# First layer's experts of a two-layer gated cross-attention block: one plain fp32 product where three rounded ones stood

## The chip, the cores and the metric

One core of one Trainium2 chip runs the whole program. The metric is device time in microseconds, from several executions of the same program; lower is better. TensorE is PE in the profile (its weight loads are PEld), VectorE is DVE, ScalarE is ACT, GpSimd is POOL and SyncE is SP.

## The reference

Two layers, each a gated cross-attention and a gated feed-forward part, over 4 × 512 tokens of width 256. The change touches the first layer's feed-forward part alone, eight experts of which each token uses one:

```python
x = hidden_states.reshape(-1, d)
router_logits = x @ Wr + br
expert_mask = jax.nn.one_hot(jnp.argmax(router_logits, axis=-1), num_experts, dtype=x.dtype)
out = jnp.zeros_like(x)
for e in range(num_experts):
    h = jax.nn.gelu(x @ W1[e] + b1[e], approximate=False)
    h = jax.nn.gelu(h @ W2[e] + b2[e], approximate=False)
    y = h @ W3[e] + b3[e]
    out = out + expert_mask[:, e:e + 1] * y
```

W1 is 256 × 1024, W2 1024 × 512 and W3 512 × 256 for each expert, everything in fp32.

## The kernel before

The program runs four phases after one another: sigmoid_attention, experts_phase, softmax_attention and last_ffn_phase. In a product of two fp32 matrices it writes each operand as a rounded high half of type float32r and a low half, the rest (x − high), also float32r. mm3 (line 48) then adds three matmuls into one PSUM bank: high × high, high × low, low × high (its lines 50 to 52, under which all phases' products stand in the profile). Where operands aren't split, a product is a single nc.tensor.matmul on fp32 operands; line 608 (probabilities times values, 4 batches × 2 × 4 calls, 512 columns, each into 32 of the array's columns) and line 586 (router logits, 32 calls, 8 columns) of the first attention are of that kind, and so are the transposes.

experts_phase: the router has given every token an expert; the tokens lie in DRAM in buckets (xs), one per expert. The tokens of an expert are cut into slots of 256 rows. PE runs one loop over all slots, in order of the experts; with this input there are 12 slots. The first slot of an expert is here called an opening slot, and an expert with tokens a visit. The other engines loop over the experts, and inside over an expert's slots.

What a slot does, in the order written out for PE in slot (lines 1738 to 1773):
- W1: for each of 8 blocks m of the first hidden layer, 2 products (over 256 inputs) of 256 columns. They go to one of four PSUM banks in turn (RING).
- transpose_slot(s + 1), line 1734: four transposes of the next slot's rows xg.
- W2: for each of 4 blocks, 8 products of 256 columns. For the first block all products with W2's high half come before those with its low half (lines 1756 to 1761), so that the low half may come later.
- W3: for each of 4 blocks of the hidden layer, 2 products of 256 columns, into banks 4 and 5.

ACT writes each of the 12 blocks per slot as h32 = Gelu(PSUM + bias) (line 1566), and the high halves of the transposed rows (gT_hi, line 1582), of three quarters of W1 (line 1593), of W2 (line 1572) and of W3 (line 1576). DVE writes high and low halves of each h block (lines 1633 and 1635), the low half of the rows (gT_lo, line 1618), the first quarter of W1's high half (line 1700) and all low halves of weights (lines 1707, 1641, 1644). The splits of W2 are put at fixed blocks of the opening slot (W2_AT, W3_AT), those of W1 for the next expert behind the last slot of the present one. DVE also adds the last bias to the result in finish (line 1627), at block 9 of the following slot or, for an expert's last slot, behind the split of W1. POOL fetches the rows xg of slot s + 1 once slot s's rows are transposed (line 1517), fetches b3 and stores the results (line 1521). SP loads the raw weights of a visit as soon as the last visit's have been split (lines 1483, 1490, 1492); in the last visit it loads w1_raw once more (line 1497) and copies the second layer's weights inside DRAM (fw, line 1501). The phase ends when all of them are done.

Of the kernel before, what the change touches and what calls it, by code (L numbers as in the profile page):

```python
# [1412 lines left out]
def experts_phase(nc, k, io):  # L1413
# [4 lines left out]
    with ctx:  # L1418
# [18 lines left out]
        b3_ld, zero_ok, w1q_ok, fw_st = sem("b3_ld"), sem("zero_ok"), sem("w1q_ok"), sem("fw_st")  # L1437
# [4 lines left out]
        gT_hi, gT_lo = sb("gT_hi", [P, C, SLOT], F32R), sb("gT_lo", [P, C, SLOT], F32R)  # L1442
        h32 = sb("h32", [P, RING, SLOT])
        h_hi, h_lo = sb("h_hi", [P, BL, SLOT], F32R), sb("h_lo", [P, BL, SLOT], F32R)
        yo = sb("yo", [P, HALVES, D])
        b_ld, w1_ld, w3_ld, xg_ld, y_st = (sem(n) for n in ("b_ld", "w1_ld", "w3_ld", "xg_ld", "y_st"))
        w1h_ok, w1l_ok, w2h_ok, w2l_ok, w3h_ok, w3l_ok = (sem(n) for n in ("w1h_ok", "w1l_ok", "w2h_ok", "w2l_ok", "w3h_ok", "w3l_ok"))
        gt_done, gh_ok, gl_ok, hb_done = (sem(n) for n in ("gt_done", "gh_ok", "gl_ok", "hb_done"))

        gelu_ok, hh_ok, hl_ok, y_done, y_used = (sem(n) for n in ("gelu_ok", "hh_ok", "hl_ok", "y_done", "y_used"))
# [23 lines left out]
        def _(sp):  # L1476
            sp.dma_start(b12[:], io["b12"]).then_inc(b_ld, 16)
            sp.wait_ge(meta_ok, 3)
            with sp.Fori(0, E0) as e:
                n0, n1, v = slots_of(nc, sp, meta, e, SLOTS0)  # L1480
                with sp.If(n0 < n1):
                    sp.wait_ge(w1l_ok, v * W1Q + 1)
# [3 lines left out]
                    for h in range(2):  # L1486

                        sp.wait_ge(w2l_ok, v * M2 + (h + 1) * M2 // 2)
                        cols = slice(h * M2 // 2, (h + 1) * M2 // 2)
                        sp.dma_start(w2_raw[:, cols], io["W2"][bass.ds(e * P, P), cols]).then_inc(w2_ld[h], 16)  # L1490
                    sp.wait_ge(w3l_ok, v + 1)
# [4 lines left out]
            sp.wait_ge(w1l_ok, visits * W1Q + 1)  # L1496
# [64 lines left out]
        def _(act):  # L1561
            def slot(s, v=None):
                for m in range(BL):
                    act.wait_ge(hb_done, s * BL + m + 2)
                    act.wait_ge(hl_ok, s * BL + m + 1)
                    nc.scalar.activation(h32[:, m % RING], ps[:, HIDDEN_BANKS[m % RING], 0:SLOT], ACT.Gelu,  # L1566
                                         bias=be[:, m:m + 1]).then_inc(gelu_ok, 1)
                    if v is not None and m in W2_AT:
                        i = W2_AT.index(m)
                        if i % 2 == 0:  # L1570
                            act.wait_ge(w2_ld[i // 2], 16 * v + 16)
                        nc.scalar.activation(w2_hi[:, i], w2_raw[:, i], ACT.Copy).then_inc(w2h_ok, 1)
# [11 lines left out]
            act.sem_inc(gelu_ok, RING)  # L1584

# [13 lines left out]
            with act.Fori(0, E0) as e:  # L1599
                n0, n1, v = slots_of(nc, act, meta, e, SLOTS0)  # L1600
                with act.If(n0 < n1):
                    nc.scalar.activation(warm[:, 1:2], warm[:, 0:1], ACT.Gelu)
                    act.wait_ge(be_ok, v + 1)
                    slot(n0, v)
                    with act.If(n0 + 1 < n1):
                        with act.Fori(n0 + 1, n1) as s:
                            slot(s)
                    act.end_ifs()
# [6 lines left out]
        def _(dve):  # L1615
            def transposed(s):
                dve.wait_ge(gh_ok, s + 1)
                nc.vector.tensor_tensor(gT_lo[:], ps[:, 0, :].rearrange("p (c n) -> p c n", c=C), f32(gT_hi[:]),  # L1618
                                        ALU.subtract).then_inc(gl_ok, 1)

# [8 lines left out]
            def slot(s, v, first):  # L1629
                for m in range(BL):  # L1630
                    n = s * BL + m
                    dve.wait_ge(gelu_ok, n + 1 + RING)
                    nc.vector.tensor_copy(h_hi[:, m], h32[:, m % RING]).then_inc(hh_ok, 1)  # L1633
                    dve.wait_ge(hh_ok, n + 1)
                    nc.vector.tensor_tensor(h_lo[:, m], h32[:, m % RING], f32(h_hi[:, m]), ALU.subtract).then_inc(hl_ok, 1)  # L1635
                    if m == FINISH_AT and not first:
                        finish(s, v + 2)
                    if first and m in W2_AT:
                        i = W2_AT.index(m)
                        dve.wait_ge(w2h_ok, v * M2 + i + 1)  # L1640
                        nc.vector.tensor_tensor(w2_lo[:, i], w2_raw[:, i], f32(w2_hi[:, i]), ALU.subtract).then_inc(w2l_ok, 1)
                    if first and m == W3_AT:
                        dve.wait_ge(w3h_ok, v + 1)
                        nc.vector.tensor_tensor(w3_lo[:], w3_raw[:], f32(w3_hi[:]), ALU.subtract).then_inc(w3l_ok, 1)
                    if m == M1 - 1:
                        transposed(s + 1)

            for start, by in ((hl_ok, RING), (w1l_ok, 1), (w2l_ok, M2), (w3l_ok, 1)):
                dve.sem_inc(start, by)
# [48 lines left out]
            def first_weights(v):  # L1698
                dve.wait_ge(w1_ld, 16 * v + 16)
                nc.vector.tensor_copy(w1_hi[:, 0:Q1], w1_raw[:, 0:Q1]).then_inc(w1q_ok, 1)  # L1700
                for h in range(W1Q):
                    if h:
                        dve.wait_ge(w1h_ok, (W1Q - 1) * v + h)
                    else:
                        dve.wait_ge(w1q_ok, v + 1)
                    w = slice(h * Q1, (h + 1) * Q1)
                    nc.vector.tensor_tensor(w1_lo[:, w], w1_raw[:, w], f32(w1_hi[:, w]), ALU.subtract).then_inc(w1l_ok, 1)

            first_weights(0)
            transposed(0)  # L1710
# [18 lines left out]
        def _(pe):  # L1729
# [8 lines left out]
            def slot(s, v):  # L1738
                pe.wait_ge(gl_ok, s + 1)
                for m in range(M1):  # L1740
                    if m % Q1 == 0:
                        pe.wait_ge(w1l_ok, W1Q * v + m // Q1 + 2)
                    pe.wait_ge(gelu_ok, s * BL + m + 1)
                    for c in range(C):
                        last = mm3(nc, ps[:, HIDDEN_BANKS[m % RING], 0:SLOT], w1_hi[:, m, c], w1_lo[:, m, c], gT_hi[:, c], gT_lo[:, c], c == 0, c == C - 1)
                    last.then_inc(hb_done, 1)
                transpose_slot(s + 1)
                for m in range(M2):
                    pe.wait_ge(gelu_ok, s * BL + M1 + m + 1)
                    out = ps[:, HIDDEN_BANKS[m % RING], 0:SLOT]  # L1750
                    if m == 0:

                        pe.wait_ge(w2h_ok, v * M2 + 1)
                        for j in range(M1):
                            pe.wait_ge(hl_ok, s * BL + j + 1 + RING)
                            nc.tensor.matmul(out, w2_hi[:, m, j], h_hi[:, j], start=j == 0, stop=False)
                            nc.tensor.matmul(out, w2_hi[:, m, j], h_lo[:, j], start=False, stop=False)
                    pe.wait_ge(w2l_ok, (v + 1) * M2 + m + 1)
                    for j in range(M1):
                        if m == 0:  # L1760
                            last = nc.tensor.matmul(out, w2_lo[:, m, j], h_hi[:, j], start=False, stop=j == M1 - 1)
                        else:
                            last = mm3(nc, out, w2_hi[:, m, j], w2_lo[:, m, j], h_hi[:, j], h_lo[:, j], j == 0, j == M1 - 1)
                    last.then_inc(hb_done, 1)
                pe.wait_ge(w3l_ok, v + 2)
                pe.wait_ge(y_used, HALVES * s + 2)
                for j in range(M2):
                    pe.wait_ge(hl_ok, s * BL + M1 + j + 1 + RING)
# [431 lines left out]
```

## Time and profile before

| | |
|---|---|
| median of 3 runs | 805.08 us (804.01 to 805.99) |
| the profiled execution | 801.95 us |
| its span, first to last instruction | 800.5 us |
| mean granted clock of PE | 0.919 of full speed |
| busy: PE, PEld | 673.4, 617.8 us |
| busy: DVE, ACT, POOL | 510.5, 329.0, 227.6 us |

The busy time of an engine is the union of its records. PE's records overlap, since a matmul starts while the last one is still draining; so its rate is read from the distance between starts. The granted clock is the share of full speed that PE was allowed. In the order of time each line has the start from the beginning of the span and the duration, both in us, and in brackets how long the engine had been idle and what ended it. Records that follow each other are drawn together, with their number behind the x.

### The profile page before, as it was taken

To read this page: it belongs to the slowest core of one execution; us is meant where nothing else is said; L and a number is where in the kernel's file an instruction comes from. 1 tells how busy PE (TensorE), PEld (TensorE's weight loads), DVE (VectorE), ACT (ScalarE), POOL (GpSimd) and SP (SyncE) were. 2 spreads that over 40 slices of the span, in tenths; PEclk is the share of its full clock that TensorE was granted. 3 is DMA by queue.
4 is the path that set the end of the run, shared out by engine and by line. 5 is a ranking of instruction groups with operands and counts; after the bars stand their busy time and mean duration, and the time that the engine had idled before them with its cause. 6 is when DMAs were issued, how large, how long until landed. Compare 5 with 4: busy or idle time off the path is not lost. (4 is left out here: it accounts for less than half of the span.)

```text
span 800.5 us, 14999 instructions
## 1 busy us (share of the span) xinstructions
PE 673.4 (84%) x4947; PEld 617.8 (77%) x4948; DVE 510.5 (64%) x1280; ACT 329.0 (41%) x557; POOL 227.6 (28%) x336
## 2 busy tenths in 40 slices
PE   4798952999999999999745678597997889999996
PEld 3566652999999999999644546376997789999996
DVE  6845455788544786445768787685665775565575
ACT  7543312556333554334363544426432423343331
POOL 7531434011000110001055865366001711011053
PEclk9999965999999999999967878889998999999999
DMA  7999216755200354003841000000004411111024
GB/s 274 416 418 403 92 43 214 256 171 186 79 26 26 131 197 131 26 26 131 285 130 52 1 30 24 0 1 1 1 1 167 163 48 44 36 52 51 27 71 153
DMA packets 23140, 91.75 MB, mean 115 GB/s; under 512 B 4417, under 2 KB 8770, under 8 KB 17378
## 3 DMA queue, kind: packets, MB, share of 16 engines
q1 hardware_dynamic: 15938, 69.69, 23.7%
q0 software_dynamic: 7168, 21.63, 8.7%
q8 instruction: 18, 0.29, 0.1%
q14 instruction: 16, 0.13, 0.1%
HBM read 51.99 MB, written 45.61 MB: 122 GB/s over the span
## 5 line engine op out<-in xcount | busy, mean ns | idle before, releaser
L1566 ACT ACTIVATE e_h<-psum,e_be 128x256 f32<-128x256 f32 x144 | 66.0, 475 | 140.8 <-PE psum L52 103.7
L1633 DVE CAST e_h_hi<-e_h 128x256 fp32r<-128x256 f32 x144 | 42.0, 292 | 85.2 <-ACT e_h L1566 85.2
L1919 ACT ACTIVATE vz<-psum,fb 128x256 f32<-128x256 f32 x112 | 52.6, 477 | 100.6 <-PE psum L52 100.2
L50 PE MATMUL psum<-e_h_hi,e_w_hi 128*128 128x256 f32 x288 | 81.6, 283 | 0.0
L51 PE MATMUL psum<-e_h_lo,e_w_hi 128*128 128x256 f32 x288 | 80.9, 281 | 0.0
L52 PE MATMUL psum<-e_h_hi,e_w_lo 128*128 128x256 f32 x288 | 80.8, 281 | 0.0
L1635 DVE TENSOR_TENSOR e_h_lo<-e_h,e_h_hi 128x256 fp32r<-128x256 f32 x144 | 61.2, 425 | 4.9
L50 PE MATMUL psum<-e_gT_hi,e_w_hi 128*128 128x256 f32 x192 | 56.1, 292 | 1.6 <-DVE e_gT_lo L1618 1.6
L51 PE MATMUL psum<-e_gT_lo,e_w_hi 128*128 128x256 f32 x192 | 55.1, 287 | 0.0
L52 PE MATMUL psum<-e_gT_hi,e_w_lo 128*128 128x256 f32 x192 | 55.0, 287 | 0.0
L50 PEld LDWEIGHTS psum<-e_h_hi,e_w_hi 128*128 128x128 f32 x288 | 54.2, 188 | 0.8
L52 PEld LDWEIGHTS psum<-e_h_hi,e_w_lo 128*128 128x128 f32 x288 | 54.3, 188 | 0.0
L51 PEld LDWEIGHTS psum<-e_h_lo,e_w_hi 128*128 128x128 f32 x288 | 54.3, 188 | 0.0
L1968 DVE TENSOR_TENSOR f_h_lo<-vz,f_h_hi 128x256 fp32r<-128x256 f32 x112 | 47.7, 425 | 4.0 <-DVE f_h_hi L1966 0.2
L1521 POOL DMA_DIRECT2D ys<-e_yo x12 | 8.6, 718 | 130.9 <-DVE e_yo L1627 130.6
L50 PE MATMUL psum<-kz_hi,s_qT_hi 128*128 128x256 f32 (+1 forms) x80 | 32.3, 404 | 13.6 <-DVE s_sc L974 9.3
L813 POOL TENSOR_TENSOR s_sc<-s_sc,s_top 128x1024 f32<-128x1024 f32 x16 | 30.5, 1903 | 38.9 <-DVE s_top L980 38.9
L1966 DVE CAST f_h_hi<-vz 128x256 fp32r<-128x256 f32 x112 | 33.5, 299 | 10.6 <-ACT vz L1919 10.6
L52 PE MATMUL psum<-f_gT_hi,f_w_lo 128*128 128x256 f32 x144 | 40.2, 279 | 0.0
L50 PE MATMUL psum<-f_gT_hi,f_w_hi 128*128 128x256 f32 x144 | 40.2, 279 | 0.0
L51 PE MATMUL psum<-f_gT_lo,f_w_hi 128*128 128x256 f32 x144 | 40.1, 279 | 0.0
L50 PEld LDWEIGHTS psum<-e_gT_hi,e_w_hi 128*128 128x128 f32 x192 | 37.4, 195 | 3.1 <-issue 3.1
(425 smaller groups left out, 2283.4 us busy)
## 6 DMA issues: line engine op xcount, KB each, us to landing
e_w_raw<-in_W SPq DMA_DIRECT2D x19, 1024.0 KB, 5.1
xs<-zeros SPq DMA_DIRECT2D x18, 1024.0 KB, 18.1
ys<-zeros SPq DMA_DIRECT2D x6, 1024.0 KB, 23.9
ys<-e_yo POOLq DMA_DIRECT2D x14, 256.0 KB, 3.1
e_xg<-xs POOLq DMA_DIRECT2D x13, 256.0 KB, 3.0
e_w_raw<-in_W SPq DMA_DIRECT2D x6, 512.0 KB, 3.4
f_w_lo<-fw SPq DMA_DIRECT2D x6, 512.0 KB, 6.8
ys<-x_norm POOLq DMA_DIRECT2D x10, 256.0 KB, 2.5
```

The source lines that it names most:

```text
L50: nc.tensor.matmul(out, wh, xh, start=start, stop=False)
L51: nc.tensor.matmul(out, wh, xl, start=False, stop=False)
L52: return nc.tensor.matmul(out, wl, xh, start=False, stop=stop)
L813: nc.gpsimd.tensor_tensor(sc[:, n % 3], sc[:, n % 3], top[:, n % 2, :, None].to_broadcast([P, HEADS, KEYS]), ALU.subtract).then_inc(sub_ok, 1)
L1521: pool.dma_start(result_of(s - 1), yo[:]).then_inc(y_st, 16)
L1566: nc.scalar.activation(h32[:, m % RING], ps[:, HIDDEN_BANKS[m % RING], 0:SLOT], ACT.Gelu, bias=be[:, m:m + 1]).then_inc(gelu_ok, 1)
L1633: nc.vector.tensor_copy(h_hi[:, m], h32[:, m % RING]).then_inc(hh_ok, 1)
L1635: nc.vector.tensor_tensor(h_lo[:, m], h32[:, m % RING], f32(h_hi[:, m]), ALU.subtract).then_inc(hl_ok, 1)
L1919: nc.scalar.activation(h32[:, m % RING], ps[:, HIDDEN_BANKS[m % RING], 0:SLOT], ACT.Relu, bias=b1[:, f * MH + m:f * MH + m + 1]).then_inc( ...
L1966: nc.vector.tensor_copy(h_hi[:, m], h32[:, m % RING]).then_inc(hh_ok, 1)
L1968: nc.vector.tensor_tensor(h_lo[:, m], h32[:, m % RING], f32(h_hi[:, m]), ALU.subtract).then_inc(hl_ok, 1)
```

## The change

All high and low halves of the phase go. Weights are copied once from their raw tile into a plain fp32 tile (half of W1 on DVE and half on ACT, W2 and W3 on DVE at the start of the opening slot); Gelu writes h itself and ACT's copy of the transposed rows writes gT itself; each product is one nc.tensor.matmul on fp32 operands. Semaphores are renamed to match, and the bias addition is no longer tied to a block. The core of the diff:

```diff
-        w1_hi, w2_hi, w3_hi = sb("w1_hi", [P, M1, C, P], F32R), sb("w2_hi", [P, M2, M1, P], F32R), sb("w3_hi", [P, M2, D], F32R)
-        w1_lo, w2_lo, w3_lo = sb("w1_lo", [P, M1, C, P], F32R), sb("w2_lo", [P, M2, M1, P], F32R), sb("w3_lo", [P, M2, D], F32R)
+        w1, w2, w3 = sb("w1", [P, M1, C, P]), sb("w2", [P, M2, M1, P]), sb("w3", [P, M2, D])
         W1Q = 4
         Q1 = M1 // W1Q
-        W2_AT = (5,M1-1,M1,M1+1)
-        W3_AT = M1 + 2
-        FINISH_AT = M1+1
+        ON_VECTOR = W1Q // 2
...
@@ -1559,38 +1555,29 @@ (scalar)
-            def slot(s, v=None):
+            def slot(s):
                 for m in range(BL):
                     act.wait_ge(hb_done, s * BL + m + 2)
-                    act.wait_ge(hl_ok, s * BL + m + 1)
-                    nc.scalar.activation(h32[:, m % RING], ps[:, HIDDEN_BANKS[m % RING], 0:SLOT], ACT.Gelu,
+                    nc.scalar.activation(h[:, m], ps[:, HIDDEN_BANKS[m % RING], 0:SLOT], ACT.Gelu,
                                          bias=be[:, m:m + 1]).then_inc(gelu_ok, 1)
...
             def transposed(s):
                 act.wait_ge(gt_done, s + 1)
-                nc.scalar.activation(gT_hi[:], ps[:, 0, :].rearrange("p (c n) -> p c n", c=C), ACT.Copy).then_inc(gh_ok, 1)
+                nc.scalar.activation(gT[:], ps[:, 0, :].rearrange("p (c n) -> p c n", c=C), ACT.Copy).then_inc(g_ok, 1)
...
@@ -1626,26 +1605,18 @@ (vector)
-            def slot(s, v, first):
-                for m in range(BL):
-                    n = s * BL + m
-                    dve.wait_ge(gelu_ok, n + 1 + RING)
-                    nc.vector.tensor_copy(h_hi[:, m], h32[:, m % RING]).then_inc(hh_ok, 1)
-                    dve.wait_ge(hh_ok, n + 1)
-                    nc.vector.tensor_tensor(h_lo[:, m], h32[:, m % RING], f32(h_hi[:, m]), ALU.subtract).then_inc(hl_ok, 1)
...
+            def second_weights(v):
+
+                for i in range(M2):
+                    if i % 2 == 0:
+                        dve.wait_ge(w2_ld[i // 2], 16 * v + 16)
+                    nc.vector.tensor_copy(w2[:, i], w2_raw[:, i]).then_inc(w2_ok, 1)
+
+            def third_weights(v):
+                dve.wait_ge(w3_ld, 16 * v + 16)
+                nc.vector.tensor_copy(w3[:], w3_raw[:]).then_inc(w3_ok, 1)
...
                     dve.wait_ge(gelu_ok, n0 * BL + RING)
                     nc.vector.tensor_copy(be[:], b12[:, bass.ds(e * BL, BL)]).then_inc(be_ok, 1)
-                    slot(n0, v, True)
+
+                    dve.wait_ge(hb_done, n0 * BL + 2)
+                    second_weights(v)
+                    third_weights(v)
                     with dve.If(n0 + 1 < n1):
                         with dve.Fori(n0 + 1, n1) as s:
-                            slot(s, v, False)
+                            finish(s, v + 2)
                     dve.end_ifs()
+
+                    dve.wait_ge(g_ok, n1 + 1)
                     first_weights(v + 1)
                     finish(n1, v + 2)
...
@@ -1736,39 +1706,33 @@ (tensor)
             def slot(s, v):
-                pe.wait_ge(gl_ok, s + 1)
+                pe.wait_ge(g_ok, s + 1)
...
                     for c in range(C):
-                        last = mm3(nc, ps[:, HIDDEN_BANKS[m % RING], 0:SLOT], w1_hi[:, m, c], w1_lo[:, m, c], gT_hi[:, c], gT_lo[:, c], c == 0, c == C - 1)
+                        last = nc.tensor.matmul(ps[:, HIDDEN_BANKS[m % RING], 0:SLOT], w1[:, m, c], gT[:, c], start=c == 0, stop=c == C - 1)
                     last.then_inc(hb_done, 1)
                 transpose_slot(s + 1)
                 for m in range(M2):
                     pe.wait_ge(gelu_ok, s * BL + M1 + m + 1)
...
+                    pe.wait_ge(w2_ok, (v + 1) * M2 + m + 1)
                     for j in range(M1):
                         if m == 0:
-                            last = nc.tensor.matmul(out, w2_lo[:, m, j], h_hi[:, j], start=False, stop=j == M1 - 1)
-                        else:
-                            last = mm3(nc, out, w2_hi[:, m, j], w2_lo[:, m, j], h_hi[:, j], h_lo[:, j], j == 0, j == M1 - 1)
+                            pe.wait_ge(gelu_ok, s * BL + j + 1 + RING)
+                        last = nc.tensor.matmul(ps[:, HIDDEN_BANKS[m % RING], 0:SLOT], w2[:, m, j], h[:, j], start=j == 0, stop=j == M1 - 1)
                     last.then_inc(hb_done, 1)
...
                     for t in range(HALVES):
-                        r = slice(t * P, (t + 1) * P)
-                        last = mm3(nc, ps[:, 4 + t, 0:D], h_hi[:, M1 + j, r], h_lo[:, M1 + j, r], w3_hi[:, j], w3_lo[:, j], j == 0, j == M2 - 1)
+                        last = nc.tensor.matmul(ps[:, 4 + t, 0:D], h[:, M1 + j, t * P:(t + 1) * P], w3[:, j], start=j == 0, stop=j == M2 - 1)
```

## Rows read from the trace of the kernel before

**Rows 1.** The page: busy tenths and granted clock in 40 slices of 20 us.

```profile
PE   4798952999999999999745678597997889999996
...
PEclk9999965999999999999967878889998999999999
```

**Rows 2.** Stretches cut at the transposes; columns: stretch, length, each engine busy, granted clock.

```profile
133.30:144.40 11.10, 9.48 (x52) 9.09 (x53) 5.76 (x16) 5.68 (x10) 1.98 (x3) 0.61 0.87 289
144.40:166.20 21.80, 21.38 (x175) 20.60 (x174) 17.40 (x36) 13.53 (x24) 2.06 (x3) 1.00 0.67 235
166.20:188.70 22.50, 21.29 (x174) 20.54 (x173) 18.27 (x38) 13.36 (x24) 2.07 (x3) 1.00 0.56 190
...
211.20:231.80 20.60, 20.60 (x175) 20.41 (x174) 9.59 (x29) 6.27 (x13) 1.43 (x2) 1.00 0.08 25
...
379.40:396.40 17.00, 15.75 (x126) 14.80 (x124) 13.64 (x25) 8.65 (x15) 0.00 (x0) 1.00 1.00 335
```

**Rows 3.** Order of time on PE inside a repeating slot; columns: start us, us, engine, line.

```profile
249.90 0.28 PE L51 MATMUL psum<-e_gT_lo,e_w_hi 128*128 128x256 f32 x1
...
252.15 0.28 PE L52 MATMUL psum<-e_gT_hi,e_w_lo 128*128 128x256 f32 x1
252.27 0.60 PE L1734 MATMUL psum<-ident,e_xg 128*128 128x128 f32 x4
```

**Rows 4.** Order of time on PE where an expert opens.

```profile
167.94 0.28 PE L1757 MATMUL psum<-e_h_lo,e_w_hi 128*128 128x256 f32 x1
169.15 0.39 PE L1756 MATMUL psum<-e_h_hi,e_w_hi 128*128 128x256 f32 x1 [0.94 <-DVE e_h_lo L1635]
```

**Rows 5.** Groups of the phase on DVE: busy us, mean ns, idle before.

```profile
L1635 DVE TENSOR_TENSOR e_h_lo<-e_h,e_h_hi 128x256 fp32r<-128x256 f32 x144 | 61.2, 425 | 4.9
L1633 DVE CAST e_h_hi<-e_h 128x256 fp32r<-128x256 f32 x144 | 42.0, 292 | 85.2 <-ACT e_h L1566 85.2
L1641 DVE TENSOR_TENSOR e_w_lo<-e_w_raw,e_w_hi 128x1024 fp32r<-128x1024 f32 x24 | 29.3, 1222 | 2.5 <-ACT e_w_hi L1572 2.5
```

**Rows 6.** Order of time at the start of the phase on DVE and PE.

```profile
135.10 0.69 DVE L1618 TENSOR_TENSOR e_gT_lo<-psum,e_gT_hi 128x512 fp32r<-128x512 f32 x1 [4.03 <-ACT e_gT_hi L1582]
...
136.04 0.57 PE L50 MATMUL psum<-e_gT_hi,e_w_hi 128*128 128x256 f32 x1 [1.60 <-DVE e_gT_lo L1618]
```

**Rows 7.** Order of time at the end of the phase on DVE and PE.

```profile
394.89 2.50 DVE L1707 TENSOR_TENSOR e_w_lo<-e_w_raw,e_w_hi 128x512 fp32r<-128x512 f32 x4
...
396.07 0.28 PE L52 MATMUL psum<-e_w_hi,e_h_lo 128*128 128x256 f32 x1
```

**Rows 8.** The plain products of lines 608 and 586: durations (least, median, most), then order of time.

```profile
L608 PE MATMUL psum<-a_prob,a_vz x64: 592/605/617, 32.2 to 97.2; 128*32 128x512 f32 x64
...
32.20 0.62 PE L608 MATMUL psum<-a_prob,a_vz 128*32 128x512 f32 x1
...
32.66 0.61 PE L608 MATMUL psum<-a_prob,a_vz 128*32 128x512 f32 x4
...
32.22 0.14 PEld L608 LDWEIGHTS psum<-a_prob,a_vz 128*32 128x32 f32 x5
...
58.02 1.95 PE L586 MATMUL psum<-a_rw,a_xrT 128*128 128x8 f32 x16
```

**Rows 9.** Order of time on PE, rounded matmuls of 512 columns.

```profile
29.82 0.39 PE L52 MATMUL psum<-xT_hi,a_w_lo 128*128 128x512 f32 x1
...
30.98 0.39 PE L51 MATMUL psum<-xT_lo,a_w_hi 128*128 128x512 f32 x1
```

**Rows 10.** Order of time on PE at the half clock, rounded matmuls of 256 columns.

```profile
137.48 0.41 PE L50 MATMUL psum<-e_gT_hi,e_w_hi 128*128 128x256 f32 x1
...
138.76 0.41 PE L50 MATMUL psum<-e_gT_hi,e_w_hi 128*128 128x256 f32 x1
```

**Rows 11.** Granted clock around line 586, columns as in rows 2.

```profile
112.50:116.20 3.70, 3.58 (x16) 3.48 (x16) 0.04 (x1) 0.00 (x0) 1.71 (x2) 0.50 0.30 106
57.90:60.00 2.10, 1.95 (x16) 1.86 (x16) 0.69 (x1) 0.66 (x2) 0.00 (x0) 0.98 0.98 406
```

More of the change, by code:

```diff
@@ L1441, in experts_phase @@
         xg = sb("xg", [P, HALVES, D])
-        gT_hi, gT_lo = sb("gT_hi", [P, C, SLOT], F32R), sb("gT_lo", [P, C, SLOT], F32R)
-        h32 = sb("h32", [P, RING, SLOT])
-        h_hi, h_lo = sb("h_hi", [P, BL, SLOT], F32R), sb("h_lo", [P, BL, SLOT], F32R)
+        gT = sb("gT", [P, C, SLOT])
+        h = sb("h", [P, BL, SLOT])
         yo = sb("yo", [P, HALVES, D])
         b_ld, w1_ld, w3_ld, xg_ld, y_st = (sem(n) for n in ("b_ld", "w1_ld", "w3_ld", "xg_ld", "y_st"))
-        w1h_ok, w1l_ok, w2h_ok, w2l_ok, w3h_ok, w3l_ok = (sem(n) for n in ("w1h_ok", "w1l_ok", "w2h_ok", "w2l_ok", "w3h_ok", "w3l_ok"))
-        gt_done, gh_ok, gl_ok, hb_done = (sem(n) for n in ("gt_done", "gh_ok", "gl_ok", "hb_done"))
-        gelu_ok, hh_ok, hl_ok, y_done, y_used = (sem(n) for n in ("gelu_ok", "hh_ok", "hl_ok", "y_done", "y_used"))
+        w1v_ok, w1a_ok, w2_ok, w3_ok = (sem(n) for n in ("w1v_ok", "w1a_ok", "w2_ok", "w3_ok"))
+        gt_done, g_ok, hb_done = (sem(n) for n in ("gt_done", "g_ok", "hb_done"))
+        gelu_ok, y_done, y_used = (sem(n) for n in ("gelu_ok", "y_done", "y_used"))
         ps, meta, xs, ys = k["ps"], k["meta0"], k["xs0"], k["ys0"]
@@ L1481, in _ @@
                 with sp.If(n0 < n1):
-                    sp.wait_ge(w1l_ok, v * W1Q + 1)
+                    sp.wait_ge(w1v_ok, v * ON_VECTOR + 1)
+                    sp.wait_ge(w1a_ok, v * (W1Q - ON_VECTOR) + 1)
                     sp.dma_start(w1_raw[:], io["W1"][bass.ds(e * P, P)]).then_inc(w1_ld, 16)
                     sp.wait_ge(xg_ld, 16)
[L1486 to L1491, printed above, removed]
+                    for a in range(2):
+                        sp.wait_ge(w2_ok, v * M2 + (a + 1) * M2 // 2)
+                        cols = slice(a * M2 // 2, (a + 1) * M2 // 2)
+                        sp.dma_start(w2_raw[:, cols], io["W2"][bass.ds(e * P, P), cols]).then_inc(w2_ld[a], 16)
+                    sp.wait_ge(w3_ok, v + 1)
                     sp.dma_start(w3_raw[:], io["W3"][bass.ds(e * P, P)]).then_inc(w3_ld, 16)
@@ L1590, in first_weights @@
                 act.wait_ge(w1_ld, 16 * v + 16)
-                for h in range(1, W1Q):
-                    w = slice(h * Q1, (h + 1) * Q1)
-                    nc.scalar.activation(w1_hi[:, w], w1_raw[:, w], ACT.Copy).then_inc(w1h_ok, 1)
+                for a in range(ON_VECTOR, W1Q):
+                    w = slice(a * Q1, (a + 1) * Q1)
+                    nc.scalar.activation(w1[:, w], w1_raw[:, w], ACT.Copy).then_inc(w1a_ok, 1)
             act.wait_ge(zero_ok, 1)
@@ L1603, in _ @@
                     act.wait_ge(be_ok, v + 1)
[L1604 to L1608, printed above, removed]
+                    with act.Fori(n0, n1) as s:
+                        slot(s)
                     first_weights(v + 1)
@@ L1627, in finish @@
                     nc.vector.tensor_tensor(yo[:, t], ps[:, 4 + t, 0:D], b3e[:], ALU.add).then_inc(y_used, 1)
-            def slot(s, v, first):
-                for m in range(BL):
-                    n = s * BL + m
-                    dve.wait_ge(gelu_ok, n + 1 + RING)
-                    nc.vector.tensor_copy(h_hi[:, m], h32[:, m % RING]).then_inc(hh_ok, 1)
-                    dve.wait_ge(hh_ok, n + 1)
-                    nc.vector.tensor_tensor(h_lo[:, m], h32[:, m % RING], f32(h_hi[:, m]), ALU.subtract).then_inc(hl_ok, 1)
[L1636 to L1648, printed above, removed]
+            def second_weights(v):
[6 more added lines that the diff above has]
+                nc.vector.tensor_copy(w3[:], w3_raw[:]).then_inc(w3_ok, 1)
+            for start, by in ((w1v_ok, 1), (w2_ok, M2), (w3_ok, 1)):
                 dve.sem_inc(start, by)
@@ L1699, in first_weights @@
                 dve.wait_ge(w1_ld, 16 * v + 16)
[L1700 to L1703, printed above, removed]
[L1704 to L1707 removed]
+                for a in range(ON_VECTOR):
+                    w = slice(a * Q1, (a + 1) * Q1)
+                    nc.vector.tensor_copy(w1[:, w], w1_raw[:, w]).then_inc(w1v_ok, 1)
             first_weights(0)
[L1710 removed]
             finish(0, 1)
```

38 lines of the change are left out of this document (11 added, 27 removed).

## The prediction

> **What bounds the kernel now.** I read the page's table of slices first: in tenths 7 to 20 of the span, which is the expert phase, the PE row is almost all nines and PEclk stands at full speed [rows 1]. So I cut that phase into stretches at the transposes of each slot. PE is busy for the whole of a slot that only repeats an expert (20.5 us out of 20.5), and for all but 1.2 us of a slot that opens a new one (21.3 out of 22.5); DVE is busy for 9.5 to 18.3 us and ACT for 6.3 to 13.5 us of them [rows 2]. Nothing but PE sets the length of a repeating slot. The next view is the order of time on PE. In the loop the matmuls' starts run evenly: 19 steps from 249.90 to 252.15 us, 118.4 ns each, which is 256 columns at 2.4 GHz (106.7 ns) and 12 ns more [rows 3]. The 0.28 us of one record is its latency, not its price. A slot has 56 products (16 of W1, 32 of W2, 8 of W3), each of three such matmuls: 168 × 0.1184 = 19.9 us. The other 0.6 us of the 20.5 are four transposes [rows 3], the restart behind them and the turn of the loop.
>
> **What is removed.** (1) Where a new expert opens, PE stands still: at 167.94 it has issued its last ready matmul, and it goes on at 169.15, because DVE, behind the splitting of W2, delivers the low halves late [rows 4]. Four opening stretches (one of them stands in the rows, from 166.2) are each 2.0 us longer than a repeating one, the last (from 379.4, without a following W1) by PE's idle time about as much, the first (144.4 to 166.2) is 1.3 us longer [rows 2]: 11.3 us in all, for six visits (four quarters of W2 are split per visit, 24 in all [rows 5]). In the new code no low half exists. DVE's four copies of 128x1024 can cost no more than the subtraction of that size, 1.22 us [rows 5]; they start after the slot's first W1 block (two products), some 0.9 us in, so the first is there at 2.1 us and the last at 5.8 us, where PE wants them from 7 us on (16 products of W1). The copy of W3 is wanted 14 us later still. So that stall goes to nothing; the cover is 5 us deep, and if it were gone a stall of at most 2 us a visit would be back. (2) At the start PE waits until DVE has written gT_lo after ACT's gT_hi: DVE starts at 135.10, as soon as ACT is done, and PE at 136.04 [rows 6]. Without DVE's step PE starts about 0.9 us earlier. (3) At the end DVE runs four low halves of W1 (394.89 to 397.39) while the last product ends at 396.35, and only then adds the bias for the last store, which the next phase waits for [rows 7]. In the new code the bias addition waits for PE alone: 1.0 us. The six copies of fw are still issued once the last visit's W1 is split, about as the last slot begins, and have a longer slot to land in. ACT's twelve Gelus a slot stay as they are, with more time between two of them. Sum removed: 13.2 us.
>
> **What is put in their place.** One plain product for three. The trace has plain fp32 products in the first attention. Its line 608 is called 32 times and has 64 matmul records, so one plain product is two records, each with a weight load of its own; line 586, called 8 times for a batch, leaves 16 [rows 8]. What does a record cost? With 512 columns it lasts 592 to 617 ns, where a rounded one of 512 columns lasts 390 to 400: one more run of 512 columns at 2.4 GHz (213 ns) [rows 8, 9]. And its second record starts 0.46 us after its first (32.20, 32.66), with three other column tiles running beside it, which leaves about 0.43 us per record behind the first load [rows 8]. So a record streams each column twice, and a plain product costs four runs of its columns where the rounded three cost three. For 256 columns the lower end is the bare stream, 4 × 106.7 = 427 ns. For the upper end I take the nearest row by length and weight load: the rounded matmul of 512 columns keeps a pitch of 230 ns (29.82 to 30.98, five steps, [rows 9]), so twice that, 460 ns. Which? The 12 ns over the bare stream appear at 2.4 GHz and not at 1.2 GHz, where the same matmul has a pitch of 213 ns (137.48 to 138.76, six steps, [rows 10]); a plain record takes a new column at just that slower rate. So I take 430 ns, near the lower end. The gain or loss per product is then 430 − 355 = +75 ns.
>
> The Trainium skill ("FP8 and Floating Point Precision", TensorE Precision Notes) says true FP32 takes four passes through the array, which speaks against this change; the durations of lines 608 and 52 agree. At today's pitch of a pass that would be 474 ns a product and the sum 66 us instead of 36.6. Its page "TensorE: Matmul & The Clock Gate" (Back-to-back issue gap) has N/2.4 + 2.5 ns for a warm matmul, 109 ns here; the trace disagrees for rounded operands (118.4), and by that rule a plain product would cost 432 ns, a sum of 37.9 us.
>
> **The sum.** A slot: 56 × 0.430 + 0.6 = 24.7 us against 20.53; twelve slots, +49.8 us. All stalls off: −13.2. The first 5.9 us of the loop run at a granted clock of 0.50 [rows 2, 10] before and, I assume, after. Net +36.6 us. The profiled execution took 801.95 us (span 800.5), the median of the runs is 805.08, 0.4% higher; so 838.6 for an execution like that, and 841.7 for the median, which I round to 842. Ends: at 427 ns +34.5 (839.6), at 460 ns 12 × (25.8 + 0.6 − 20.5) = +70 − 13 = +57 (862). What lies outside the phase, on SP, POOL and in the DMA queues, is issued in the same number; nothing there is on the path, as POOL asks for a slot's rows (line 1517) when the transposes of the slot before are done, a whole slot ahead.
>
> **Rivals.** *A record costs one run of its columns* (the other side). Place: every product of the loop. Price: two records at 118.4, 237 ns a product; a slot 13.9 us, twelve −79.8, with the stalls −93: 712 us. The point from which it decides: the loop of today, from 136.04 [rows 6] to 396.35 [rows 7], is 260.3 us, of which 246.4 are twelve slots, 11.3 stalls and 2.6 the slow start. The new one costs the same where 12 × (56p + 0.6) + 2.6 − 1.9 = 260.3, at p = 375 ns a product; below that the change is a gain. For it: the four plain transposes of 128 columns, one record each, pass in 0.60 us [rows 3]. Against: the 592 ns. 5%, in which I count that the compiler makes something else of these operands than it does on line 608.
> *The weight load isn't covered.* Two loads of 128 columns per product, at the 111 to 122 ns between records of line 586 (16 in 1.95 us, where the matmul has 8 columns [rows 8]), on top of 427: 56 × 12 × 0.22 = +148 more, about 990 us. Against: in line 608 five loads had been started by 32.34 while the first matmul ran, [rows 8], and each rounded matmul hides a load of 128 columns in its 118 ns. 3%.
> *The granted clock falls in the loop.* Line 586, plain, ran at 0.50 in its last burst (112.5 to 116.2) but at 0.98 in its first (57.9 to 60.0) [rows 11]: so the product alone doesn't set it, but no long run of plain products is in the trace. If plain products kept the clock at 1.2 GHz, a product would be 0.854 us and the phase 12 × 48.4: 1125 us. 3%.
> *New waits stay or come in openings* (PE on w2_ok or on be): up to 2 us a visit, with the 11.3 not recovered, 853 us, inside the range. 8%.
> *The pitch passes the upper end.* Line 52's pitch a pass (118.4), four times, would be 474 ns and 871 us. 4%.
>
> **How the numbers follow.** The forecast, with its ends, has 76%, the openings 8%, a pitch above the end 4%, one run per record 5%, uncovered loads 3%, the lower clock 3%, and 1% is an even result. 0.3% (2.4 us) is about what a measurement of this kernel tells from no change. Slower by more: 76 + 8 + 4 + 3 + 3 = 0.94; within: 0.01; faster: 0.05. The range 835 to 862 takes in the bounds 839.6 and 862, the openings, and 4 us below for the spread of runs and the 0.6 us of restarts; the far rivals stay outside it.
>
> **What would show it.** In the changed profile: 1344 matmul records of plain products (12 × 56 × 2) at starts 213 to 230 ns apart; DVE's busy time down by over 100 us (the 144 pairs of line 1633 and 1635 alone are 103 us, [rows 5]), ACT's by some 30 (W2 and W3 leave it); repeating slots of 24.5 to 26.4 us and opening slots of the same length; PE's first product near 135.1; PEclk at full speed from the same moment on. A pitch near 0.118 a record, an opening slot 2 us longer than the others, or PEclk at 0.50 inside the loop would each prove a step wrong.

## The result and the profile after

The changed kernel takes 840.81 us (840.47 to 842.26, 4 runs) where the kernel before, run beside it, takes 805.54 us (804.01 to 808.39, 4 runs). The ratio is 1.0435, with a 95% interval of 1.0401 to 1.0469: 35 us slower. The profiled execution took 842.26 us (span 840.8).

First the page, with the rows that answer to [rows 1], and its groups of PE in the phase:

```profile
PE 718.0 (85%) x4275; PEld 630.5 (75%) x4276; DVE 374.6 (45%) x958; ACT 299.3 (36%) x520; POOL 227.8 (27%) x336
...
PE   4798727999999999999955577776997879999997
...
DVE  6755642120000210000228788685665666655656
...
PEclk9999957999999999999986887798998989999999
...
L1728 PE MATMUL psum<-e_h,e_w 128*128 128x256 f32 x768 | 167.7, 379 | 0.0
...
L1719 PE MATMUL psum<-e_gT,e_w 128*128 128x256 f32 x384 | 87.9, 389 | 1.1 <-ACT e_gT L1568 1.1
...
L1735 PE MATMUL psum<-e_w,e_h 128*128 128x256 f32 x192 | 43.4, 379 | 0.0
```

PE is busier, DVE has lost 136 us of work and is nearly idle in the middle of the phase. PE has 768 + 384 + 192 = 1344 records for 672 products, two each. The granted clock is full (2.4 GHz) from the eighth slice to the end of the phase, as before.

Then the phase in stretches from transposes to transposes, as in [rows 2]: the first part of a slot, two opening stretches, a repeating one, the rest of the last slot.

```profile
130.10:142.30 12.20, 11.10 (x36) 8.97 (x37) 2.59 (x4) 5.41 (x10) 2.00 (x3) 0.66 0.89 302
142.30:166.90 24.60, 24.60 (x117) 21.67 (x116) 5.61 (x11) 8.56 (x17) 2.22 (x3) 1.00 0.61 224
166.90:191.50 24.60, 24.60 (x117) 21.67 (x116) 4.92 (x10) 8.55 (x17) 2.19 (x3) 1.00 0.49 172
216.20:240.80 24.60, 24.60 (x118) 21.66 (x117) 0.85 (x2) 6.25 (x13) 1.43 (x2) 1.00 0.07 21
413.00:430.95 17.95, 17.93 (x86) 15.45 (x83) 1.18 (x3) 3.96 (x8) 0.00 (x0) 1.00 0.81 256
```

All slots have one length, 24.61 us, opening or not. PE is never idle in them. The idle 1.2 us of [rows 2] and the stall of [rows 4] are gone.

The order of time, around an opening, at the start and at the end of the phase:

```profile
131.27 0.60 ACT L1568 ACTIVATE e_gT<-psum 128x512 f32<-128x512 f32 x1 [5.35 <-PE psum L1704]
...
132.31 10.18 PE L1719 MATMUL psum<-e_gT,e_w 128*128 128x256 f32 x32 [1.08 <-ACT e_gT L1568]
...
159.80 0.86 DVE L1606 TENSOR_TENSOR e_yo<-psum,e_b3e 128x256 f32<-128x256 f32 x2 [13.85 <-PE psum L1735]
...
160.03 7.07 PE L1719 MATMUL psum<-e_gT,e_w 128*128 128x256 f32 x32
...
161.81 0.17 DVE L1683 COPY e_be<-e_b 128x12 f32 x1 [1.15 <-issue]
...
162.08 2.53 DVE L1613 COPY e_w<-e_w_raw 128x1024 f32<-128x1024 f32 x4
...
166.94 0.60 PE L1704 MATMUL psum<-ident,e_xg 128*128 128x128 f32 x4
...
167.37 0.81 PE L1728 MATMUL psum<-e_h,e_w 128*128 128x256 f32 x3
...
427.31 3.62 PE L1735 MATMUL psum<-e_w,e_h 128*128 128x256 f32 x16
...
430.53 0.86 DVE L1606 TENSOR_TENSOR e_yo<-psum,e_b3e 128x256 f32<-128x256 f32 x2 [15.34 <-PE psum L1735]
```

The pitch of a record is read from the row at 160.03: 32 records in 7.07 us, the last one draining for 0.38, so 31 steps of 0.2158 us. A product costs 431.7 ns. The four copies of W2 start at 162.08 and are done at 164.61, 2.8 us before W2's first product at 167.37.

Where the time went, in the two profiled executions: the loop from first product to last lasts 298.6 us (132.31 to 430.93) instead of 260.3, +38.3; from the transposes to the first product 2.19 instead of 2.72 us, −0.5; from the last product to the next phase's first 8.49 instead of 9.73 us, −1.2. Together +36.5. The unchanged code was 3.2 us shorter ahead of it and 6.9 us longer behind it in this pair. That is spread from execution to execution: in the executions profiled below, the code ahead of the phase's transposes took 128.7 to 133.6 us (133.3 before, 130.1 here) and the code behind the phase 392.0 to 397.1 us (394.4 before, 401.3 here); two kernels with the new loop had 394.7 and 395.3 us behind it.

### The profile page after: what moved, and what is told of

Its sections match the earlier page's. It is cut to its first block and busy times, and to the rows that moved or that the text cites. A ratio compares the mean times of both kernels' runs of the same rounds, so it can differ in the third digit from the quotient of the medians.

```text
span 840.8 us, 12887 instructions
## 1 busy us (share of the span) xinstructions
PE 718.0 (85%) x4275; PEld 630.5 (75%) x4276; DVE 374.6 (45%) x958; ACT 299.3 (36%) x520; POOL 227.8 (27%) x336
## 5 line engine op out<-in xcount | busy, mean ns | idle before, releaser
L1728 PE MATMUL psum<-e_h,e_w 128*128 128x256 f32 x768 | 167.7, 379 | 0.0
L1728 PEld LDWEIGHTS psum<-e_h,e_w 128*128 128x128 f32 x768 | 145.0, 190 | 19.2
L1883 ACT ACTIVATE vz<-psum,fb 128x256 f32<-128x256 f32 x112 | 52.6, 476 | 106.7 <-PE psum L52 101.9
L1719 PE MATMUL psum<-e_gT,e_w 128*128 128x256 f32 x384 | 87.9, 389 | 1.1 <-ACT e_gT L1568 1.1
L1719 PEld LDWEIGHTS psum<-e_gT,e_w 128*128 128x128 f32 x384 | 75.0, 196 | 12.2 <-issue 1.5
L1735 PE MATMUL psum<-e_w,e_h 128*128 128x256 f32 x192 | 43.4, 379 | 0.0
L1735 PEld LDWEIGHTS psum<-e_w,e_h 128*128 128x128 f32 x192 | 36.5, 190 | 5.0
L50 PE MATMUL psum<-xT_hi,sw_hi 128*128 128x256 f32 (+1 forms) x128 | 38.0, 296 | 1.4 <-issue 0.9
L1133 PE MATMUL psum<-ident,s_sc 128*128 128x128 f32 x128 | 19.3, 300 | 21.5 <-POOL s_sc L817 18.8
L51 PE MATMUL psum<-xT_lo,sw_hi 128*128 128x256 f32 (+1 forms) x128 | 36.5, 285 | 0.0
L52 PE MATMUL psum<-xT_hi,sw_lo 128*128 128x256 f32 (+1 forms) x128 | 36.4, 284 | 0.0
```

Of the source, the lines that this page charges most:

```text
L50: nc.tensor.matmul(out, wh, xh, start=start, stop=False)
L51: nc.tensor.matmul(out, wh, xl, start=False, stop=False)
L52: return nc.tensor.matmul(out, wl, xh, start=False, stop=stop)
L1133: last = nc.tensor.transpose(ps[:, 4 + j // 4, (j % 4) * P:(j % 4 + 1) * P], sc[:, n % 3, 2 * j:2 * j + 2, :].rearrange("p h n -> p (h n)" ...
L1719: last = nc.tensor.matmul(ps[:, HIDDEN_BANKS[m % RING], 0:SLOT], w1[:, m, c], gT[:, c], start=c == 0, stop=c == C - 1)
L1728: last = nc.tensor.matmul(ps[:, HIDDEN_BANKS[m % RING], 0:SLOT], w2[:, m, j], h[:, j], start=j == 0, stop=j == M1 - 1)
```

## The experiments

Expectations were written before each kernel ran. The first four shared 17 runs of the kernel before (median 801.0 us), the last four 16 (799.91 us).

**1. Splitting moved instead of removed (e1_pool_low).** The kernel before; POOL writes the low halves of W2 and W3, which DVE wrote.

```diff
+            def low_weights(v):
+                for i in range(M2):
+                    pool.wait_ge(w2h_ok, v * M2 + i + 1)
+                    nc.gpsimd.tensor_tensor(w2_lo[:, i], w2_raw[:, i], f32(w2_hi[:, i]), ALU.subtract).then_inc(w2l_ok, 1)
...
-                    if first and m in W2_AT:
...
-                    if first and m == W3_AT:
```

> The kernel before, with the low halves of W2 and W3 written by POOL instead of DVE; every product keeps its three rounded matmuls. Theory A (two things moved the time of the change: each plain product costs 432 ns where three rounded ones cost 355, and the opening slots lost their stall): the stall of the opening slots goes alone, all twelve slots take 20.5 us, and the time falls by about 11 us, to 794. Rival B (the openings wait for the raw weights or for ACT, not for DVE's subtractions): the opening slots stay at 22.5 us and the time at 805. Rival C (POOL's 1.9 us per subtraction comes too late, or slows DVE beside it): a new stall of about the same size, 803 to 810.

It came out at 837.74 us, ratio 1.0467 (1.0433 to 1.0501), far above what any of the three theories gave. Opening slots took 29.1 us instead of 22.5, repeating ones 20.5 as before. The order of time at an opening of this kernel (the matmuls between left out) and PE's waits over the phase (total, times, longest):

```profile
168.28 0.43 DVE L1643 TENSOR_TENSOR e_h_lo<-e_h,e_h_hi 128x256 fp32r<-128x256 f32 x1
168.39 4.90 POOL L1526 TENSOR_TENSOR e_w_lo<-e_w_raw,e_w_hi 128x1024 fp32r<-128x1024 f32 x2 [2.23 <-ACT e_w_hi L1580]
...
168.62 2.48 DVE L1641 CAST e_h_hi<-e_h 128x256 fp32r<-128x256 f32 x1
...
171.13 2.44 DVE L1643 TENSOR_TENSOR e_h_lo<-e_h,e_h_hi 128x256 fp32r<-128x256 f32 x1
...
173.49 0.28 DVE L1641 CAST e_h_hi<-e_h 128x256 fp32r<-128x256 f32 x1
...
173.62 0.39 PE L1757 MATMUL psum<-e_h_hi,e_w_hi 128*128 128x256 f32 x1 [3.75 <-DVE e_h_lo L1643]
...
PE psum L1757 <- DVE e_h_lo L1643: 21.8, 8, 3.8
PE psum L50 <- POOL e_w_lo L1526: 5.7, 8, 1.1
PE psum L50 <- POOL e_w_lo L1528: 4.7, 6, 1.3
```

POOL's subtraction takes 2.4 us, twice DVE's 1.22 [rows 5]. That was thought of. The larger part was not: a DVE cast that takes 0.28 us alone took 2.48, and the subtraction behind it 2.44 instead of 0.43, each about as long as the POOL instruction beside it (2.45). So DVE, relieved of 37 us of work, delivered later, and PE waited longer for DVE (21.8 us) than for POOL (10.4). The Trainium skill ("SBUF — State Buffer", SBUF: two separate sides) says that DVE and GpSimd share a port pair by a lock: a GpSimd instruction, or a DVE instruction of the kinds that need the pair (two inputs in SBUF, or a 2-port mode), holds it to its end, and the other is blocked. This trace agrees, 2.48 us for a cast. So this kernel doesn't say what the openings gain when the splitting is out of their way; the fifth and the sixth do.

**2. Only W3's products plain (e2_w3_plain).** The kernel before, with 8 of a slot's 56 products changed, and with them the splitting of W3 and of the second hidden layer.

```diff
-                        last = mm3(nc, ps[:, 4 + t, 0:D], h_hi[:, M1 + j, r], h_lo[:, M1 + j, r], w3_hi[:, j], w3_lo[:, j], j == 0, j == M2 - 1)
+                        last = nc.tensor.matmul(ps[:, 4 + t, 0:D], h3[:, j, t * P:(t + 1) * P], w3[:, j], start=j == 0, stop=j == M2 - 1)
```

> The kernel before, with W3's products alone made plain (8 of a slot's 56), fed by an unsplit copy of W3 and of the last four hidden blocks; the rest stays split. Theory A (the loss is the pitch of each plain product, in proportion to their number): 12 x 8 x (0.432 - 0.355) = +7.4 us, slots longer by 0.61 us, the stall of the opening slots unchanged, 813 us. Rival B (the loss of the change sits in waits that come with unsplit weights, or in the clock, and not in the product): no change within 2 us, or a loss much larger than 7 us.

804.22 us, ratio 1.0039 (1.0015 to 1.0063), +3.2 us where theory A gave +7.4; the loop grew by 4.3 us, to 264.7. Its group on PE, with 192 records for 96 products:

```profile
L1770 PE MATMUL psum<-e_w,e_h 128*128 128x256 f32 x192 | 43.4, 379 | 0.0
```

They start 216 ns apart, as in the changed kernel, so the price doesn't depend on how much of the loop is plain. But a slot grew by 0.40 us (20.93 for 20.53) and not by 8 × 77 ns = 0.62. The missing 0.2 us is at the turn of PE's loop between W3 and the next W1. The order of time there, in the kernel before and in this one:

```profile
246.25 0.28 PE L52 MATMUL psum<-e_w_hi,e_h_lo 128*128 128x256 f32 x1
246.49 0.38 PE L50 MATMUL psum<-e_gT_hi,e_w_hi 128*128 128x256 f32 x1
246.71 0.28 PE L51 MATMUL psum<-e_gT_lo,e_w_hi 128*128 128x256 f32 x1
```

```profile
222.89 1.03 PE L1770 MATMUL psum<-e_w,e_h 128*128 128x256 f32 x4
223.57 0.47 PE L50 MATMUL psum<-e_gT_hi,e_w_hi 128*128 128x256 f32 x1
223.87 0.28 PE L51 MATMUL psum<-e_gT_lo,e_w_hi 128*128 128x256 f32 x1
```

Before, two steps take 244 and 220 ns where 118 is usual, 0.23 us more than needed. Here the last plain record starts at 223.54 and W1's second record 0.33 us later, which is one plain and one rounded pitch (216 and 118 ns): nothing is lost. Opening slots stayed 1.8 us longer than repeating ones. That wait belongs to W2's and the first hidden layer's splitting, which this kernel keeps.

**3. Half the columns per record (e3_half_columns).** The changed kernel; each product of W2 in two of 128 columns, so that twice as many weight loads serve the same columns.

```diff
-                        last = nc.tensor.matmul(ps[:, HIDDEN_BANKS[m % RING], 0:SLOT], w2[:, m, j], h[:, j], start=j == 0, stop=j == M1 - 1)
+                        last = nc.tensor.matmul(ps[:, HIDDEN_BANKS[m % RING], 0:P], w2[:, m, j], h[:, j, 0:P], start=j == 0, stop=j == M1 - 1)
+                    for j in range(M1):
+                        last = nc.tensor.matmul(ps[:, HIDDEN_BANKS[m % RING], P:SLOT], w2[:, m, j], h[:, j, P:SLOT], start=j == 0, stop=j == M1 - 1)
```

> The changed kernel, with each W2 product issued as two of 128 columns (four matmul records instead of two, as many columns, twice the weight loads). Theory A (a record costs two runs of its columns and 2.7 ns, the load is hidden behind it): records 109 ns apart, 32 x (4 x 0.1094 - 0.432) = +0.18 us a slot, +2 us in all, 843. Rival B (with so few columns the 128-column weight load is the bound, at the 111.6 ns seen between records of line 586): +0.46 us a slot, +5.6 us, 846. Rival C (loads are partly uncovered in any plain product, so that the 216 ns hold a share of load time): over 120 ns between records, +1.5 us a slot and more, 859 or above.

840.44 us, ratio to the kernel before 1.0499 (1.0459 to 1.0538); slots of 25.09 us, 0.48 more than 24.61, and a loop of 304.4 us, 5.8 more. The median shows less of that: 39.4 us over the kernel before, where the changed kernel was 35.3 over it in its own comparison. The groups:

```profile
L1728 PE MATMUL psum<-e_h,e_w 128*128 128x128 f32 x768 | 93.6, 275 | 0.0
L1730 PE MATMUL psum<-e_h,e_w 128*128 128x128 f32 x768 | 93.6, 275 | 0.0
L1719 PE MATMUL psum<-e_gT,e_w 128*128 128x256 f32 x384 | 88.0, 389 | 1.1 <-ACT e_gT L1568 1.1
```

The small records are 111.7 ns apart: 128 of them are 14.29 us, against 64 × 0.2158 = 13.81, which is the 0.48. Two streams of 128 columns are 106.7 ns. So at 256 columns there is room for nearly two weight loads, and the rival of uncovered loads is out by experiment too. At 128 columns the pitch is at the 111 ns of line 586's smallest records [rows 8], which have 8 columns and so hold little but the load. That the load sets it is the likely reading.

**4. The same kernel with one rounded pass (e4_one_pass).** The changed kernel with its operand tiles of type float32r; everything else stays. **8. The same in bf16 (e8_one_pass_bf16).** The edit of the fourth; the eighth has BF16 for F32R.

```diff
-        w1, w2, w3 = sb("w1", [P, M1, C, P]), sb("w2", [P, M2, M1, P]), sb("w3", [P, M2, D])
+        w1, w2, w3 = sb("w1", [P, M1, C, P], F32R), sb("w2", [P, M2, M1, P], F32R), sb("w3", [P, M2, D], F32R)
```

> The changed kernel with its tiles of type float32r: one rounded matmul for each plain product; the low parts of all products of the phase are left out. Theory A (nothing but PE's product time sets a slot in the changed kernel): the records fall to 118 ns, PE's need of a slot from 24.2 to 6.6 us, and another bound shows, ACT's 12 Gelus with their latency, at 8 to 11 us a slot; the loop falls from 298.6 us to 100 to 130, the time to 640 to 675. Rival B (waits for weights or for Gelu already hold the changed kernel's slots near 24.6 us): the slots shrink by less than half, the time stays above 720.

> The changed kernel with bf16 tiles: one bf16 matmul for each product (everything below bf16 precision is left out). It measures what the 12 ns are that a rounded matmul of 256 columns keeps above its bare stream. Theory A (they come with reading 4-byte columns at the full clock; plain records, which take columns at half the rate, keep only 2.7 ns): a run of W2's matmuls is spaced 109 to 110 ns. Rival B (any matmul with a weight load of 128 columns behind it keeps them): 118 ns.

665.4 and 663.4 us, one execution each, with 672 records for 672 products. Of the first the groups of ACT and of PE's W1, of the second a run of W2 in the order of time and the group of its weight loads:

```profile
L1561 ACT ACTIVATE e_h<-psum,e_be 128x256 fp32r<-128x256 f32 x144 | 59.3, 485 | 31.9 <-PE psum L1728 19.5 <-PE psum L1719 12.1
...
L1719 PE MATMUL psum<-e_gT,e_w 128*128 128x256 f32 x192 | 34.1, 323 | 13.1 <-issue 10.1 <-ACT e_h L1561 1.9 <-ACT e_gT L1568 1.1
```

```profile
222.78 2.35 PE L1728 MATMUL psum<-e_h,e_w 128*128 128x256 bf16 x20
...
L1728 PEld LDWEIGHTS psum<-e_h,e_w 128*128 128x128 bf16 x384 | 38.1, 101 | 6.3
```

The rounded pass keeps its pitch of 118.4 ns in W2 when it stands alone. Slots shrink to 8.8 to 9.7 us (the second stretch to 11.8), the loop to 115.9. Now PE is no longer the only bound: W1's block of two products would pass in 0.24 us, but a Gelu of ACT takes 0.485 us, and at each turn of the loop PE stands idle for up to 1.0 us in which the profile names nothing that it waits for (the 10.1 us of "issue"). With bf16 the pitch is (2.35 − 0.28) / 19 = 0.109 us. So the 12 ns over the bare stream go with float32r operands: a bf16 record has 2.5 ns, and a plain record, 215.8 ns for two streams, has 2.5 ns too, once for both. What about these operands costs the 12 ns isn't shown; with bf16 the rate of bytes is halved, and a weight load takes 101 ns instead of 196. The number of passes, not the waits, carries the phase: one pass, three and four give loops of 116, 246 (the sixth kernel) and 299 us.

**5. The stall removed without the change (e5_two_blocks).** The kernel before; at W2 the first two blocks, not one, take their high halves first, and DVE's subtractions of W2 stand behind the last block of the first hidden layer, with ACT's high halves of W2 moved to match.

```diff
-                for m in range(M2):
+                for m in range(2):
                     pe.wait_ge(gelu_ok, s * BL + M1 + m + 1)
                     out = ps[:, HIDDEN_BANKS[m % RING], 0:SLOT]
-                    if m == 0:
...
+                    pe.wait_ge(w2h_ok, v * M2 + m + 1)
+                    for j in range(M1):
+                        if m == 0:
                             pe.wait_ge(hl_ok, s * BL + j + 1 + RING)
...
+                        nc.tensor.matmul(out, w2_hi[:, m, j], h_hi[:, j], start=j == 0, stop=False)
+                        nc.tensor.matmul(out, w2_hi[:, m, j], h_lo[:, j], start=False, stop=False)
```

> The kernel before with another order where an expert opens: PE takes the high-half matmuls of W2's first two blocks before the low-half ones of either, and DVE subtracts W2's low halves behind the last W1 block's split instead of before blocks 6 and 7; the number and kind of all operations stay. Theory A (the opening stall is DVE's subtraction standing ahead of the splits of h that PE waits for): the opening slots shrink from 22.5 to about 21 us, 5 x 1.5 = 7 to 8 us in all, ratio to before 0.990. Rival B (the stall comes from ACT or the weight loads): opening slots stay at 22.5 us and the ratio at 1.000. Rival C (the new order makes blocks 2 and 3 wait): opening slots above 22.5.

795.99 us (790.87 to 798.82, 11 runs) against 799.91, ratio 0.9940 (0.9916 to 0.9964). A stretch to an opening and, for comparison, a repeating one; then the longest wait of PE left at an opening:

```profile
165.50:186.90 21.40, 21.08 (x174) 20.47 (x173) 18.24 (x40) 13.27 (x24) 2.04 (x3) 1.00 0.61 204
208.00:228.60 20.60, 20.60 (x175) 20.41 (x175) 9.59 (x29) 6.28 (x14) 1.43 (x2) 1.00 0.08 25
```

```profile
168.21 0.39 PE L1764 MATMUL psum<-e_h_hi,e_w_hi 128*128 128x256 f32 x1 [0.16 <-DVE e_h_lo L1639]
```

Opening slots fell from 22.5 to 21.2 us and the loop from 260.3 to 253.0: two thirds of the 11.3 us of stalls came back by order alone, with all three rounded passes kept. The medians show less of it, −3.9 us, where theory A had 0.990 for the ratio; in the profiled execution the stretch from the last product to the next phase's first was 1.3 us longer than in the profile of before (11.0 for 9.7; the last section has a reason). This kernel is 0.6% faster than the one before, clear of the noise, and faster than the changed one.

**6. Three rounded passes, nothing split (e6_three_same).** The kernel of the fourth run, whose products are three matmuls of the same two tiles, with the factor of one third taken in by the Gelu's scale and the last addition. It has as many matmuls and as many weight loads as the kernel before.

```diff
+                        last = mm3(nc, ps[:, HIDDEN_BANKS[m % RING], 0:SLOT], w2[:, m, j], w2[:, m, j], h[:, j], h[:, j], j == 0, j == M1 - 1)
```

> The changed kernel, but each product is three rounded matmuls of the same, once rounded operands (a third of the sum is used; the low parts of the phase's products are left out): PE's work of the kernel before with the other engines' work of the changed one. Theory A (the change is the sum of +77 ns for each of 672 products and of stalls that go): repeating and opening slots alike at 20.5 us (168 x 0.1184 + 0.6), the loop at 246.4 + 2.6 = 249 us, 11 us under the kernel before and 50 us under the changed one: 791 if the kernel before is at 803, ratio 0.985. Rival B (the rounded matmuls' pace in the kernel before was held back by the splitting beside them): slots clearly under 20.3 us. Rival C (the openings of the kernel before waited for raw weights or ACT, which this kernel still does): opening slots at 22.5.

785.04 us (781.71 to 786.04), ratio 0.9809 (0.9774 to 0.9845). Two of its groups on PE, of 384 and 192 products' first passes:

```profile
L50 PE MATMUL psum<-e_h,e_w 128*128 128x256 f32 x384 | 108.9, 284 | 0.0
...
L50 PE MATMUL psum<-e_gT,e_w 128*128 128x256 f32 x192 | 55.4, 289 | 1.0 <-ACT e_gT L1568 1.0
```

This cuts the change in two. Removing the splitting alone makes the loop 246.4 us, −14.0; all slots take 20.28 us, so 3.0 us of it are the turn of the loop (0.25 a slot), which shows no gap here, and 11.0 the stalls of the openings. Putting plain products for the three passes makes it 298.6, +52.3: a slot grows by 4.33 us, which is 56 × (431.7 − 3 × 118.1) ns, with 118.1 ns for the mean pitch of this kernel's 168 rounded records in a slot.

**7. The cover of the copies taken away (e7_late_copies).** The changed kernel; DVE's copies of W2 and W3 begin once W1's products of the opening slot are done.

```diff
-                    dve.wait_ge(hb_done, n0 * BL + 2)
+                    dve.wait_ge(hb_done, n0 * BL + M1 + 1)
```

> The changed kernel, with DVE's copies of W2 and W3 begun only when all of W1's products are done, so that the cover named in the prediction is gone. Theory A (the copies are hidden by 5 us of W1's products): with 0.69 us for a copy of 128x1024 PE waits some 0.3 to 0.8 us at the first W2 block of each opening slot, 2 to 5 us in all; other slots stay at 24.61. Rival B (the copies never mattered, PE starts W2 late enough anyway): all slots stay at 24.61.

840.65 us in one execution. Its total says nothing at this size, its slots do: opening ones took 25.38, repeating ones 24.61 us, +0.77 each, within what theory A gave. A copy and PE's waits in the phase:

```profile
168.52 0.69 DVE L1613 COPY e_w<-e_w_raw 128x1024 f32<-128x1024 f32 x1 [5.33 <-PE psum L1719]
...
PE psum L1728 <- DVE e_w L1613: 3.0, 6, 0.5
```

One copy of 0.69 us lies on the path of each of six openings and the other three run beside the first block's products. In the changed kernel all of this is covered.

## Why the prediction was right

The forecast was 842.0 us and slower; 840.81 us came. By its steps:

- **Four runs of the columns per plain product.** Right, and it decides the sign. Forecast 430 ns, measured 431.7 ns; ends 427 and 460. The reading of line 608's durations and second starts [rows 8] carried over from 512 columns into 32 columns of the array to full products of 256 columns. The 12 ns over the bare stream were argued to stay away at the slower rate of taking columns, as at the half clock [rows 10]. They did stay away (2.5 ns are left), but no run shows that this is the reason: kernel 8 lost them too, with bf16 at the full rate of columns. By the rule of the Trainium skill ("TensorE: Matmul & The Clock Gate", Back-to-back issue gap) a record that streams its 256 columns twice would take 215.8 ns; the trace gives that to the tenth. It also gives the bf16 record's 109 ns and misses the rounded one's 118.4.
- **The rest of a slot, 0.6 us.** Mis-sized: it is 24.61 − 56 × 0.4317 = 0.43 us, about what the four transposes take (166.94 to 167.37). The turn of the loop costs nothing visible once plain records run up to it, as in kernel 2. Over twelve slots −2.0 us; the pitch, 1.7 ns too low, takes +1.1 back. A slot: 24.61 for 24.7.
- **Stalls, −11.3 us.** Right. Slots are equal in the changed kernel, and kernel 6 gives −11.0 with the turn set apart.
- **Copies.** Hidden, as forecast. Each costs 0.69 us, not up to 1.22, and the four start 2.05 us behind W1's first product, not 0.9, as DVE reaches the copy of the biases ahead of them only at 161.81, behind 1.15 us in which it waits for nothing that the profile shows. They are still done 2.8 us ahead of W2's first product. Uncovered they cost 0.77 us a visit (kernel 7); the bound was 2 us.
- **Start, −0.9 us.** Mis-sized: −0.53. DVE's 0.69 us step and the hand over to it went, but PE now follows ACT by 0.44 us (131.87 to 132.31), where it followed DVE by 0.25 [rows 6].
- **Tail, −1.0 us.** Mis-sized: −1.24. I counted from the last split to the last product and left out that DVE did both halves' additions behind it; now the first half's addition (430.53) runs beside the last products.
- **The slow clock at the start.** The first 5.9 us run at a granted clock of 0.50, as assumed, but 14 records at 427 instead of 216 ns cost 3.0 us more and the first one another 0.16, where the rounded passes lost 2.6. The working carried 2.6 over.
- **The sum.** Forecast +36.6 us; the loop, the start and the tail give +36.5 in the profiled pair, the medians +35.3. The mechanism is right; that the sum agrees to 0.1 us is luck, since errors of both signs (the pitch +1.1, the slow clock +0.5, the start +0.4, the rest of a slot −2.0, the tail −0.2) cancel almost wholly.

The rivals: one run per record (712 us) and the load uncovered (990 us) fell with the pitch of 216 ns, and so did the pitch above the end (871 us); the low clock (1125 us) fell with a granted clock of 1.00 in every slot behind the first, and new waits in openings (853 us) with equal slots. Kernel 7 brings the last of these about, at 0.77 us a visit.

## What to carry to other kernels

Where PE bounds a stretch, price a change of operand type by the pitch of its records, counted from the trace, before any saving on other engines: here the splitting that three rounded passes need cost 14 us of the loop in all, and the plain products in their place 52. Ask then whether the saving can be had without the price; reordering two blocks brought back 7 of those 14 us in the loop. And don't move a large elementwise instruction to POOL beside short DVE instructions on the path without measuring those.

## What the runs showed of the hardware that I had not expected

- A POOL subtraction of 128x1024 (2.4 us) stretches the DVE instruction beside it from 0.28 or 0.43 to 2.4 us (kernel 1).
- At 256 columns and full clock a record's pitch is 118.4 ns with float32r operands, 109 ns with bf16, and 215.8 ns plain, where each streams twice. At 128 columns a plain record takes 111.7 ns.
- The turn of PE's loop costs the kernel before 0.25 us a slot, and nothing in kernel 6, which has the same number of matmuls and fewer waits between them. Whether the waits or something else in PE's queue make the gap wasn't tried.
- The end of the phase has a bound of its own, which a shorter last slot uncovers. The six copies of fw are issued about as the last slot begins, and the last of them lands some 21 to 22 us after its issue; the store of the slot before, issued beside them, takes 19 to 20 us instead of some 3, and the last addition needs its buffer. In the changed kernel that store lands before the last product. In kernel 6, with slots 4.3 us shorter, the addition waits 1.3 us for it, and the tail is 10.1 us, not 8.5:

```profile
361.10 3.82 SPq L1497 DMA_DIRECT2D fw<-in_fw  x6
...
363.63 0.91 POOL L1517 DMA_DIRECT2D ys<-e_yo  x1
...
383.48 0.76 DVE L1606 SCALAR_TENSOR_TENSOR e_yo<-psum,e_b3e 128x256 f32<-128x256 f32 x2 [13.96 <-DMA ys<-e_yo]
```

In kernel 4, whose last slot is shorter still, the same addition comes 11.8 us behind the last product, and the tail is 22.7 us. In kernel 5 it is the last store that lands late, 3.8 us after its issue instead of 2.5. That the copies cause all this is the likely reading; no run left them out.
